# Conv block on one core: activations between the two convolutions stored by parity of rows, two taps of a column in one matmul of 128 rows

## The reference

```python
g   = groupnorm(x, 32 groups of 2 channels)            # eps 1e-5
out = conv3x3(g, quantised(w1)) + b1                   # 64 -> 64 channels, padding 1
out = relu(batchnorm(out, gamma1, beta1))              # statistics over all 32 images
out = conv3x3(out, quantised(w2)) + b2
out = relu(batchnorm(out, gamma2, beta2) + g)
result = x + out
```

## Time and profile before

| | |
|---|---|
| median of three runs | 536.12 us |
| the profiled execution, its own time | 536.91 us |
| span in its trace, first to last instruction | 535.1 us |
| PE busy | 392.8 us, 9,501 matmuls |
| DVE busy | 462.4 us |
| ACT busy | 331.4 us |
| HBM read and written | 61.48 MB and 35.50 MB |

### The profile page before, as it was taken

The page is one execution under the profiler, slowest core; times in us unless marked ns, Lnnn a source line. Parts: engine busy times, 40 slices in busy tenths (PEclk is TensorE's granted clock), DMA queues, the critical chain, the costliest instruction groups (busy, mean ns, idle before and its releaser), DMA issues.

```text
span 535.1 us, 20532 instructions
## 1 busy us (share of the span) xinstructions
PE 392.8 (73%) x9501; PEld 351.2 (66%) x9501; DVE 462.4 (86%) x593; ACT 331.4 (62%) x350; POOL 83.3 (16%) x147
## 2 busy tenths in 40 slices
PE   3999999999999999999999999999991000000000
PEld 1899889999999787899888998888880000000000
DVE  7999989999999757988988887798877999798995
ACT  3898799999999955765555566655515923544200
POOL 2027226666551500000000000000000000000000
PEclk9999999999999999999999999999996555555555
DMA  8934874433333000143333300000066999999997
GB/s 267 358 129 132 269 265 159 181 129 131 129 135 129 8 8 6 46 171 152 129 127 128 124 2 4 4 3 4 2 244 208 355 429 381 431 429 428 432 429 318
DMA packets 21965, 99.21 MB, mean 185 GB/s; under 512 B 6520, under 2 KB 8952, under 8 KB 16504
## 3 DMA queue, kind: packets, MB, share of 16 engines
q1 hardware_dynamic: 20256, 81.55, 40.4%
q10 hardware_dynamic: 1624, 16.36, 7.2%
HBM read 61.48 MB, written 35.50 MB: 181 GB/s over the span
## 4 chain that ended last, share of the span: by engine, by line
PE 72%; DMA 14%; DVE 10%; issue 2%; ACT 1%; SPq 0%; DVEq 0%
PE conv_ps L994 70%; DMA xa<-in_x_dram 11%; DVE slots L948 4%; DVE slots L951 3%; DMA out_dram<-xa 2%; DMA slots<-in_x_dram 1%; DVE xa L951 1%; DVE conv_ps L948 1%; PE conv_ps L957 1%; ACT split L435 0%; DVE gn_tup L674 0%; PE wt_ps L994 0%; PE stat_ps L994 0%; PE conv_ps L992 0%; DVE bn_tup L775 0%
## 5 line engine op out<-in xcount | busy, mean ns | idle before, releaser
L994 PE MATMUL conv_ps<-split,wmat 64*64 64x385 f16 (+3 forms) x9144 | 377.7, 324 | 2.1 <-ACT split L435 1.4
L994 PEld LDWEIGHTS conv_ps<-split,wmat 64*64 64x64 bf16 x9144 | 339.1, 107 | 37.6 <-issue 2.3
L469 ACT ACTIVATE slots<-conv_ps,par,evac_scale 128x784 f32<-128x784 f32 x124 | 123.7, 998 | 95.3 <-PE conv_ps L994 93.4
L775 DVE BATCH_NORM_STATS2 bn_tup<-slots 128x6 f32<-128x392 f32 x166 | 81.9, 555 | 15.6 <-ACT slots L469 15.6
L600 ACT ACTIVATE slots<-slots,skip_b,bn_w 128x3136 f32<-128x3136 f32 (+3 forms) x20 | 45.8, 2340 | 47.6 <-DVE slots L951 29.9
L674 DVE BATCH_NORM_STATS2 gn_tup<-slots 128x6 f32<-128x448 f32 x112 | 61.8, 612 | 0.9 <-DMA slots<-in_x_dram 0.9
L742 DVE TENSOR_TENSOR split<-slots,split 128x3136 f16<-128x3136 f32 (+4 forms) x36 | 57.2, 1607 | 3.5 <-ACT slots L449 0.9
L744 DVE SCALAR_TENSOR_TENSOR split<-slots,split 128x3248 f16<-128x3248 f32 (+3 forms) x18 | 53.6, 2979 | 2.3
L728 DVE TENSOR_SCALAR slots<-slots,bn_w 128x3248 f32<-128x3248 f32 (+3 forms) x18 | 30.4, 1688 | 21.4 <-ACT split L427 20.9
L427 ACT ACTIVATE split<-slots,bn_w 128x3248 f16<-128x3248 f32 x14 | 43.2, 3083 | 0.0
L477 ACT ACTIVATE xa<-conv_ps,par,evac_scale 128x784 bf16<-128x784 f32 x40 | 39.7, 994 | 0.0
(11 more groups left out here) (124 smaller groups left out, 214.4 us busy)
## 6 DMA issues: line engine op xcount, KB each, us to landing
out_dram<-slots SPq DMA_DIRECT2D x13, 1568.0 KB, 15.2
slots<-in_x_dram SPq DMA_DIRECT2D x51, 392.0 KB, 5.6
split<-in_x_dram ACTq DMA_DIRECT2D x5, 1568.0 KB, 23.4
slots<-in_x_dram SPq DMA_DIRECT2D x4, 1568.0 KB, 7.3
y_spill<-slots SPq DMA_DIRECT2D x3, 1624.0 KB, 7.3
slots<-y_spill SPq DMA_DIRECT2D x3, 1624.0 KB, 7.0
y_spill<-slots SPq DMA_DIRECT2D x3, 1568.0 KB, 5.8
slots<-y_spill SPq DMA_DIRECT2D x3, 1568.0 KB, 13.5
```

What stands on the lines that cost most here:

```text
L469: nc.scalar.activation(dst, src, ACT.Identity, bias=bias, scale=scale, accum_out=total).then_inc(evacuated[ph], 1)
L775: ins = nc.vector.bn_stats(bn_tup[:, 2 * (n - first) + s, :], rows[s])
L994: return nc.tensor.matmul(bank[:, r0:r1, w0:w1], lhs, rows[:, top + r0:top + r1, w0 + kx - 1:w1 + kx - 1], start=n == 0 and part is hi_all ...
```

## The change

Convolution 1 writes rows by **parity**: its output has (parity of the row, channel) in the partitions, and along them (pair of rows, image, column). Convolution 2 then finds the rows 2r and 2r+1 of both images in the two partition halves at one place. For an output row of either parity, two of the three taps of a column of the filter read rows 2r and 2r+1: they become one matmul with 128 rows of the array and 64 columns (`parity_tile`, taps = 0). The third tap reads a neighbour in one partition half: a matmul with 64 rows and 64 columns (taps = 1). e is the parity of the output row, b the image.

Further: no halo copies and no extra row (29 rows become 28, 3,248 elements 3,136), SP's waits for them are gone, ACT waits for the evacuation in their place; the matmuls of convolution 1 read every second row; `evacuate` writes (and in the pieces of `IN_PSUM`, phase 2 writes and reads) runs of 56 elements with a step of 112; the pieces of a first pair are whole bands of rows; `wmat[1]` has 12 blocks in place of 9, filled by two DVE instructions of 64 partitions; `squares` gets memory of its own; `IN_PSUM` is handled in 8 parts of 392 elements and stored in four transfers of 784.

```diff
-                sp.wait_ge(evacuated[0], NQ * (t + 1))
-                if t >= 1:
-                    sp.wait_ge(halo_done, 32 * t)
-                sp.dma_start(v[C:P, :, 0, :], v[0:C, :, J, :]).then_inc(halo_done, 16)
-                sp.dma_start(v[0:C, :, 0, :], v[C:P, :, 1, :]).then_inc(halo_done, 16)
+                sp.wait_ge(evacuated[0], NQ * (t + 1))
...
-                    sc.wait_ge(halo_done, 32 * (PAIR2[t] + 1))
+                    sc.wait_ge(evacuated[0], NQ * (PAIR2[t] + 1))
...
-            first, stop = ((0, 9), (9, 16), (16, 23), (23, KB))[j]
-            return [flat(v[:, :, first:stop])]
+            first, stop = (((0, 15), (15, 29), (29, 43), (43, H)), ((0, 16), (16, 30), (30, 44), (44, H)))[ph][j]
+            return ap[:, first * W:stop * W]
...
-                dst = round_rows(slot_of(ph, t), ph, q)
-                src, bias, scale = conv_ps[:, BUF[q], :, 0:CH], par[:, 3 * ph:3 * ph + 1], evac_scale[:, ph:ph + 1]
+                dst = by_parity(slot_of(ph, t)[:, 2 * q * CH:2 * (q + 1) * CH])
+                src = bank_rows(conv_ps[:, BUF[q], :, 0:CH])
...
-    PARTS = [NQ + 1 if u == IN_PSUM else len(CUTS[u]) - 1 for u in range(NP)]
+    PARTS = [2 * NQ if u == IN_PSUM else len(CUTS[u]) - 1 for u in range(NP)]
...
-                nc.vector.tensor_scalar(wmat[1][:, :, :].rearrange("p t o -> p (t o)"), wt_ps[:, 0:NT], pow2[:, 0:1], None,
-                                        ALU.mult).then_inc(wmat_ready, 1)
+                for half, first in ((slice(0, C), 3), (slice(C, P), 0)):
+                    ins = nc.vector.tensor_scalar(wmat[1][half, first:first + 9, :].rearrange("p t o -> p (t o)"), wt_ps[half, 0:NT],
+                                                  pow2[half, 0:1], None, ALU.mult)
+                ins.then_inc(wmat_ready, 1)
...
+            def one_tile(t, n, part, q, a, b, last):
...
+                top = 2 * RB * q + b + ky - 1
+                return nc.tensor.matmul(bank[:, r0:r1, w0:w1], wmat[0][C * a:C * a + C, ky * 3 + kx, :],
+                                        rows[:, top + 2 * r0:top + 2 * r1 - 1:2, w0 + kx - 1:w1 + kx - 1],
+                                        start=n == 0 and part is hi_all, stop=last)
+
+            def parity_tile(t, kx, taps, part, q, e, b, first, last):
+                first_row, base, rows_of = ((0, 6, slice(0, P)), (0, 3, slice(0, P)), (-1, 0, slice(C, P)), (1, 9, slice(0, C)))[2 * taps + e]
+                rows = by_parity(part[rows_of, t % 2])[:, b]
+                bank = bank_of(1, t, q, e)[C * b:C * b + C, 0:CH].rearrange("p (r w) -> p r w", w=W)
+                w0, w1 = max(0, 1 - kx), min(W, W + 1 - kx)
+                top = RB * q + first_row
+                r0, r1 = max(0, -top), min(RB, J - top)
+                return nc.tensor.matmul(bank[:, r0:r1, w0:w1], wmat[1][rows_of, base + kx, :],
+                                        rows[:, top + r0:top + r1, w0 + kx - 1:w1 + kx - 1], start=first, stop=last)
+
+            def taps_of_part(ph, t, q, part):
+                if ph == 0:
+                    for n in range(9):
+                        for a in range(2):
+                            for b in range(2):
+                                mm = one_tile(t, n, part, q, a, b, n == 8 and part is lo_all)
+                    return mm
+                for kx in (1, 0, 2):
+                    for taps in range(2):
+                        for e in range(2):
+                            for b in range(2):
+                                mm = parity_tile(t, kx, taps, part, q, e, b, part is hi_all and kx == 1 and taps == 0,
+                                                 part is lo_all and kx == 2 and taps == 1)
+                return mm
```

More of the change, by code:

```diff
@@ L116, in conv_block_kernel @@
         ytotal = part(2)
-        squares = [part(CH).bitcast(BF16).rearrange("p (s m) -> p s m", s=2) for _ in range(2)]
         neg_round = part(1)[0:C]
-        wmat = [sb(f"wmat{n}", [P, 9, C], BF16) for n in (1, 2)]
+        wmat = [sb("wmat1", [P, 9, C], BF16), sb("wmat2", [P, 12, C], BF16)]
+        squares = [sb(f"squares{n}", [P, 2, CH], BF16)[:, :, :] for n in range(2)]
         bn_avg = sb("bn_avg", [P, P], F32)
@@ L433, in hi_piece @@
                     wait_source(ph, t)
[L434 to L436 removed]
+                nc.scalar.activation(piece(hi_of(t), ph, j), piece(slot_of(ph, t), ph, j), func, bias=bias,
+                                     scale=scale).then_inc(hi_ready[ph], 1)
             def hi_and_act(t, j):
@@ L721, in act @@
                 scale, bias = (gn_s_all[:, t:t + 1], gn_b_all[:, t:t + 1]) if ph == 0 else (A1, B1)
-                views = lambda ap: [whole(ap, ph)] if j is None else piece(ap, ph, j)
+                view = lambda ap: ap if j is None else piece(ap, ph, j)
                 if not apart(ph, t, j):
@@ L769, in bn_stats @@
                         dve.wait_ge(evacuated[ph], NQ * t + q + 1)
-                        rows = [round_rows(slot_of(ph, t), ph, q)[:, s] for s in range(2)]
+                        rows = [round_rows(slot_of(ph, t), q)[:, s] for s in range(2)]
                     for s in range(2):
@@ L980, in one_tile @@
                 w0, w1 = max(0, 1 - kx), min(W, W + 1 - kx)
[L981 to L984, removed]
-                if ph == 0:
-                    rows = src[:, 0:PIX].rearrange("p (r w) -> p r w", w=W)
-                    top = J * b + RB * q + ky - 1
-                else:
-                    rows = src.rearrange("p (s r w) -> p s r w", s=2, w=W)[:, b]
-                    top = RB * q + ky
-                    if half == 0 and q == NQ - 1 and ky == 2:
-                        nc.tensor.matmul(bank[:, RB - 1, w0:w1], lhs, rows[:, 0, w0 + kx - 1:w1 + kx - 1], start=False, stop=False)
-                        r1 = RB - 1
@@ L994, in one_tile @@
-                return nc.tensor.matmul(bank[:, r0:r1, w0:w1], lhs, rows[:, top + r0:top + r1, w0 + kx - 1:w1 + kx - 1],
-                                        start=n == 0 and part is hi_all, stop=last)
+                r0 = 1 if b == 0 and q == 0 and ky == 0 else 0
+                r1 = RB - 1 if b == 1 and q == NQ - 1 and ky == 2 else RB
+                top = 2 * RB * q + b + ky - 1
+                return nc.tensor.matmul(bank[:, r0:r1, w0:w1], wmat[0][C * a:C * a + C, ky * 3 + kx, :],
+                                        rows[:, top + 2 * r0:top + 2 * r1 - 1:2, w0 + kx - 1:w1 + kx - 1],
+                                        start=n == 0 and part is hi_all, stop=last)
@@ L1015, in conv @@
                             pe.wait_ge(ready[ph], t * NQ + NQ)
-                        for n in range(9):
-                            for a in range(2):
-                                for b in range(2):
-                                    mm = one_tile(ph, t, n, part, q, a, b, n == 8 and part is lo_all)
+                        mm = taps_of_part(ph, t, q, part)
                     mm.then_inc(round_done[ph], 1)
```

87 lines of the change are left out of this document (36 added, 51 removed).

## The result

The changed kernel takes 633.47 us, the median of four runs (632.82 to 633.99), against 536.55 for the kernel before measured with it (535.52 to 537.13, four runs). The ratio is 1.1808, 95% interval 1.1785 to 1.1831: 18% slower. The forecast was 628.7 us, range 580 to 652.

A forecast was written before the change was run, and what follows sets the result against it. PE, full through both convolutions, was taken as the bound. Terms +92.2 (768 changes at 0.12 us), +0.3, -0.2, -0.1 and +0.4 sum to +92.6, added to the median 536.12: 628.7 us, range 580 to 652.

The forecast's parts named there:

- What bounds the kernel: Both convolutions: PE has no idle time; ACT and DVE are close behind in convolution 1, irrelevant in convolution 2.
- No gain from fewer matmuls: Convolution 2: 24 matmuls a part for 36, but still three steps per filter column, 18 a round; gain 0.
- 768 changes: Convolution 2: switches between 128*64 and 64*64, 12 per round, 48 per pair, 768 in all.
- 0.12 us each: Price of each change of division in convolution 2; times 768 gives +92.2 us, ends +65 and +114.
- The step made of two rows: Price per change in convolution 2, built as 0.095 gap plus 0.025 exposed weight load, 0.12 us.
- From a change of columns to one of rows: Assumed row-only changes cost like traced column changes; matmuls before convolution 1, at two clock levels, gave 0.13 us.
- No drain: Rival, convolution 2: changing only the row division costs nothing; 535.4 us, between 534 and 537; chance 0.12.
- One direction free: Rival, convolution 2: only one direction of change, say 64 to 128 rows, costs; +46, 583 us; chance 0.08.
- Exposed loads: Rival, 128-row pairs of convolution 2: second weight load can't run during the first matmul; +41 on top, 670; chance 0.03.
- Clock: Rival: PE, streaming only about two thirds of the time, falls to its slow clock; 800 us and more; chance 0.01.
- Slower evacuations: Rival: strided evacuations slow ACT in convolution 1, adding 3 to 28 us besides the forecast; chance 0.03.
- The +0.4: Phase 2, `IN_PSUM` in eight parts: DVE +1.0 us, partly hidden by the store; +0.4, between -0.5 and +1.

The follow-up runs named there:

- e4: Changed kernel with only 64-row matmuls in convolution 2, 36 a part, no changes of division, most sums in wrong rows: 537.47 us, ratio 0.9992 to the kernel before.
- e6 to e8: Kernel before plus a one-column matmul ahead of every third step of convolution 2, of 128*64, 64*128 and 128*128 respectively: 632.13, 626.18 and 626.98 us.
- e3: Changed kernel with the third tap also in 128-row matmuls, half its weights zero, so no change of division in convolution 2: 598.05 us, ratio 1.1121.
- e10: The changed kernel itself, unaltered, run and traced a second time: 632.35 us, ratio 1.1751 to the kernel before.
- e2: Changed kernel with each part's matmuls grouped by row count, the second part in reverse order, 128 changes of division for 768: 554.84 us, ratio 1.0315.
- e9: Changed kernel with convolution 1 reading seven neighbouring rows in place of every second one, sums in wrong rows: 631.65 us, ratio 1.1744.
- e5: Kernel before plus a one-column 64*64 matmul ahead of every third step of convolution 2, no change of division: 549.58 us, ratio 1.0243.

## Why the prediction was right, point by point

- **What bounds the kernel.** Right. PE alone, array full; e4 shows that everything beside PE's divisions together weighs nothing within 0.3%, and DVE and ACT only got longer waits.
- **No gain from fewer matmuls.** Right. Three steps a filter column before and after; a third fewer instructions and no halo copies gave nothing. That L992 costs nothing fits too: e4 hasn't got it and its convolution 2 is 190.1 us, 189.8 before.
- **768 changes.** Right to the count, 756 + 12 stops.
- **0.12 us each.** Measured 0.121 to 0.123 by order and by e4, 0.109 to 0.127 in the kernel before. The step made of two rows (gap 0.095, exposed load 0.025) was right because it was read off the same events: in the changed kernel 0.26 us from the second 128-row step to the 64-row one (a step and 0.095), 0.19 from the first to the second 128-row step (a step and 0.025), and 0.28 from the 64-row step to the next (a step and both). The term comes to 94.4 in place of 92.2.
- **From a change of columns to one of rows.** This was the weakest link, since no row at full clock showed it. The estimate of 0.13 from two clock levels had the right size, partly by luck: it took the change's price to be the same at the slow clock, which no run here shows. e6 to e8 show that all kinds cost nearly the same. The Trainium skill's rule ("TensorEngine Tiling (Array Packing)", Key Properties: a change of tiling mode drains TensorE) agrees with every pair of modes tried here, 64*64 against 128*64, 64*128 and 128*128: each cost 0.10 to 0.13 us.
- **The rivals.** No drain: refuted by the profile. One direction free: refuted; 64 to 128 rows is 0.28 us from start to start after one step, 128 to 64 rows 0.26 after the second of two. Exposed loads: refuted by e3. Clock: 1.00 all through convolution 2; its one fall before phase 2, at 15.0 to 18.4 us of the profiled execution, came 197 us before the first change of division in convolution 2. Slower evacuations: L457 took 1.00 us, as L469 did.
- **`IN_PSUM`.** Eight parts took DVE 9.1 us (528.12 to 537.22, the start of the next pair), as forecast, 1.0 more than before. But the store behind them on the chain took 10.2 us in place of 11.2, and from the last matmul of convolution 2 to the end the kernel took 132.3 us in place of 133.0. The +0.4 should have been 0 or less.
- **What was missed.** The forecast is 4.8 us low, and the profiled execution 5.3. Of the 5.3, 2.2 are the price of a change, 0.123 for 0.12; 3.2 are convolution 1, for which the sum had no term: 1.7 of them the slow stretch of the clock, which a second trace doesn't show, the rest stops. 0.8 is that the sum starts at the median of the kernel before, and its profiled execution was 0.8 above; phase 2 gives 1.1 back. The other three executions have no trace, so where their excess lies isn't known. Against the kernel before measured beside it, e10's ratio of 1.1751 is nearer to the forecast's 628.7 / 536.12 = 1.1727 than the first 1.1808.

## What to carry to other kernels

Before packing taps or heads into larger matmuls, count array time and changes of division separately: here the packing saved a third of the matmuls of convolution 2 and no array time, and every switch between 64*64 and 128*64 cost 0.12 us, three quarters of a step of 392 columns. If both shapes are needed, put all matmuls of one shape together (12 changes a round cost 94 us, two cost 17), or pad the odd ones to the common shape where the padding is cheaper than two changes (here a padded step at 0.163 us against 0.24). Read PE by its starts and by PEld's idle brackets, not by its busy share.

No kernel here beats the one before: with the array full and the price of a change above zero, e2, the best correct order tried, is 3% slower, and e4, without changes but with sums in the wrong rows, only equals it.

## What the runs showed of the hardware

- A change of the array's division costs about 0.12 us at full clock: 0.121 to 0.123 between 64*64 and 128*64 by order and by e4, 0.10 to 0.13 for rows, columns or both in the kernel before, in either direction, and after one column as after 392.
- Within one division everything overlaps: 128*64 matmuls, each with its own weight load on the same rows, follow at 0.163 us for 385 to 392 columns, two side by side.
- Reading float16 rows of 112 bytes with a step of two rows costs PE nothing measurable (convolution 1 191.5 us in e9, 191.4 in e10), and writing float32 runs of 56 elements with a step costs ACT nothing (1.00 us for 784 elements, before and after).
- The same kernel was granted 1.2 GHz (0.50) for 3.4 us near its start in one execution and 2.4 GHz (1.00) in another: 1.7 us more for the same 288 matmuls (13.5 us in the changed profile, 11.8 in e10).
- One column in one quarter of the array, with its weight load, costs 0.036 us in a stream of 64*64 matmuls (e5 by its time; 0.033 by convolution 2 in its trace, 202.1 us against 189.8).
